# Recurrent attention and sparse-FFN layer: two staging buffers for the attention weights, and a down projection that reads its fp32 weights in both sweeps without the bf16 copy in HBM

## What is computed

```python
xn = layernorm(x)
q, k, v = split(xn @ w_atten.T); q, k = rope(q), rope(k)
s = softmax(causal(q @ k.T / sqrt(128))) @ v  @ w_proj.T
h = silu(xn @ w_gate) * (xn @ w_up)
h = keep the 2 largest magnitudes of every 4 neighbours of h
g = silu(h @ w_down)
out = x + s * g
```

## Time and profile before

| | us |
|---|---|
| median of the 2 runs | 4018.79 (3956.82 and 4080.75) |
| the profiled execution | 3956.59 |
| its span on the slowest core (core 7) | 3955.1 |
| spans of the eight cores | 3916.9 to 3955.1 |
| TensorE busy | 2852.7 (72%) |
| VectorE busy | 1323.3 (33%) |
| granted TensorE clock, mean | 0.862 |
| moved by DMA | 433.41 MB, 109 GB/s over the span |

### The profile page before, as it was taken

How to read it: one execution, slowest core, us unless ns; L and a number is a source line. 1 busy time by engine, 2 the same in 40 slices (tenths; PEclk the granted TensorE clock), 3 DMA queues, 4 the chain that set the end, 5 groups by cost and what they waited for, 6 DMA issues and landing times.

```text
span 3955.1 us, 34701 instructions; the slowest of 8 cores (3916.9 to 3955.1 us)
## 1 busy us (share of the span) xinstructions
PE 2852.7 (72%) x12592; PEld 1212.2 (31%) x12592; DVE 1323.3 (33%) x2055; ACT 603.4 (15%) x1102; POOL 263.6 (7%) x308
## 2 busy tenths in 40 slices
PE   2287879787878787847589898888898144444598
PEld 0041414242423233213234343334343022221243
DVE  4631312223131313110265665656656111111000
ACT  1112122222212121301011111111111000000000
POOL 0000000000000000001000000100101011111001
PEclk7698989898989888879899999999999577777799
DMA  5210110202020201052655555556461788887886
GB/s 161 76 52 29 42 47 23 68 2 68 3 67 3 67 5 44 4 190 97 156 128 140 144 123 130 132 121 156 115 157 42 213 212 211 212 212 178 200 194 157
DMA packets 638887, 433.41 MB, mean 110 GB/s; under 512 B 139648, under 2 KB 598400, under 8 KB 638336
## 3 DMA queue, kind: packets, MB, share of 16 engines
q1 hardware_dynamic: 612352, 343.09, 34.0%
q0 software_dynamic: 26368, 88.10, 8.2%
HBM read 359.86 MB, written 71.30 MB: 109 GB/s over the span
## 4 chain that ended last, share of the span: by engine, by line
PE 45%; DMA 30%; DVE 14%; issue 6%; SPq 3%; ACT 2%; DVEq 0%; ACTq 0%; POOLq 0%
DMA arena<-wd 13%; PE ps L689 11%; PE ps L345 7%; PE ps L395 6%; DMA d_hT<-arena 5%; PE ps L441 4%; PE ps L797 4%; DMA arena<-d_wdb 4%; PE ps L458 3%; PE ps L464 3%; PE ps L429 3%; DVE arena L476 3%; SPq L66 3%; PE ps L533 2%; DMA arena<-wvT 2%
## 5 line engine op out<-in xcount | busy, mean ns | idle before, releaser
L689 PE MATMUL ps<-arena 128*128 128x512 bf16 x4096 | 959.0, 393 | 34.4 <-DVE arena L665 24.4
L797 PE MATMUL ps<-arena 128*128 128x512 bf16 x2048 | 490.9, 403 | 387.2 <-DVE arena L774 324.5
L689 PEld LDWEIGHTS ps<-arena 128*128 128x128 bf16 x4096 | 411.1, 102 | 527.9 <-issue 90.6
L345 PE MATMUL ps<-arena 128*128 128x512 bf16 x1536 | 378.5, 403 | 58.7 <-DVE arena L325 58.7
L797 PEld LDWEIGHTS ps<-arena 128*128 128x128 bf16 x2048 | 209.8, 103 | 668.0 <-issue 451.0
L476 DVE RECIPROCAL arena<-ps 1x512 f32<-1x512 f32 x32 | 107.1, 3346 | 755.5 <-PE ps L458 755.5
L445 ACT ACTIVATE arena<-ps 128x512 bf16<-128x512 f32 x384 | 229.3, 597 | 314.4 <-PE ps L441 310.1
L345 PEld LDWEIGHTS ps<-arena 128*128 128x128 bf16 x1536 | 156.0, 102 | 274.8 <-issue 113.8
L395 PE MATMUL ps<-arena 128*128 128x256 bf16 x2048 | 231.7, 274 | 0.0
L819 DVE TENSOR_TENSOR arena<-arena 128x512 f32<-128x512 f32 x32 | 22.2, 693 | 614.8 <-DMA arena<-d_s 347.7
L395 PEld LDWEIGHTS ps<-arena 128*128 128x128 bf16 x2048 | 203.3, 99 | 27.8
(11 more groups left out here) (71 smaller groups left out, 1839.8 us busy)
## 6 DMA issues: line engine op xcount, KB each, us to landing
arena<-wgu SPq DMA_DIRECT2D x128, 1024.0 KB, 15.1
arena<-wd SPq DMA_DIRECT2D x32, 2048.0 KB, 29.5
d_wdb<-arena POOLq DMA_DIRECT2D x16, 2048.0 KB, 18.8
arena<-d_wdb SPq DMA_DIRECT2D x16, 2048.0 KB, 15.5
arena<-xT SPq DMA_DIRECT2D x4, 4096.0 KB, 14.5
arena<-wkT SPq DMA_DIRECT2D x8, 2048.0 KB, 8.8
arena<-wvT SPq DMA_DIRECT2D x8, 2048.0 KB, 8.8
arena<-wqT SPq DMA_DIRECT2D x8, 2048.0 KB, 8.7
```

The lines of the kernel that those rows point to most:

```text
L345: tok = E("tensor", lambda e, f=f, h2=h2, bank=bank, tile=tile, wv_=wv_: e.matmul(ps[bank][:], wv_[:, f, h2 * 128:(h2 + 1) * 128], xnv[:, ...
L689: tok = E("tensor", lambda e, f=f, tc=tc, bank=bank, gv=gv: e.matmul(ps[bank][:], xnv[:, f, tc * 128:(tc + 1) * 128], gv[:, f, :], start=( ...
L797: tok = E("tensor", lambda e, ic=ic, bank=bank, wdv=wdv: e.matmul(ps[bank][:], wdv[:, ic, :], hTv[:, ic, :], start=(ic == 0), stop=(ic == ...
```

## The change

It has two parts.

**Attention weights.** The one staging buffer becomes two (`wstag2`), used in turn (`(3g + wi) % 2`), each with its own `stag_free` entry. `wfree` becomes the last projection matmul of each kind instead of the last TensorE instruction of the group. Waits on `stag_free` in the output projection become waits on both entries.

**Down projection.** Both sweeps now load the fp32 weights and cast them; the bf16 copy `d_wdb` is neither written nor read. The two staging buffers become three, used in turn (`(2 fc + hf) % 3`).

```diff
-    wstag = A.alloc(NF * 256)
+    wstag2 = [A.alloc(NF * 256) for _ in range(2)]
...
+            sl = (3 * g + wi) % 2
+            t_l = kb.dma("sync", wstag2[sl][:].rearrange("p (c d) -> p c d", d=256),
+                         srcw, sem,
+                         [stag_free.get(sl)] + (xn_done if g == 0 else []))
+            t_c = E("vector", lambda e, wbf=wbf, sl=sl: e.tensor_copy(
+                wbf[:], wstag2[sl][:]), [t_l, wfree[nm]], "DVE")
+            stag_free[sl] = t_c
...
-        wfree = {"q": group_pe_tail, "k": group_pe_tail, "v": group_pe_tail}
+        wfree = {"q": q_last_mm, "k": k_last_mm, "v": v_last_mm}
...
-    wd_st2 = [A.alloc(NIC * 64) for _ in range(2)]
+    wd_st2 = [A.alloc(NIC * 64) for _ in range(3)]
...
-            if sweep == 0:
+            if True:
...
+                    hfs = (2 * fc + hf) % 3
                     t_wl = kb.dma("sync",
-                                  wd_st2[hf][:].rearrange("p (c d) -> p c d", d=128),
-                                  srcw, "dWD0" if hf == 0 else "dWD1",
-                                  [wdst_free.get(hf)] + (ph4a_tail if fc == 0 else []))
+                                  wd_st2[hfs][:].rearrange("p (c d) -> p c d", d=128),
+                                  srcw, ["dWD0", "dWD1", "dWDB0"][hfs],
+                                  [wdst_free.get(hfs)] + (ph4a_tail if sweep == 0 and fc == 0 else []))
...
-                        [t_wl, wd_read.get(fc - 2), wd_spill.get(fc - 2),
-                         ph4a_tail[2] if fc < 2 else None], "DVE")
-                    wdst_free[hf] = t_c
+                        [t_wl, wd_read.get(fc - 2),
+                         ph4a_tail[2] if sweep == 0 and fc < 2 else None], "DVE")
+                    wdst_free[hfs] = t_c
...
-                t_ws = kb.dma("gpsimd", wdbv[:, :, fc * 128:(fc + 1) * 128],
-                              wd_b[par][:].rearrange("p (c d) -> p c d", d=128),
-                              "dWDS0" if par == 0 else "dWDS1", casts)
-                wd_spill[fc] = t_ws
-            else:
-                t_wc = kb.dma("sync",
-                              wd_b[par][:].rearrange("p (c d) -> p c d", d=128),
-                              wdbv[:, :, fc * 128:(fc + 1) * 128],
-                              "dWDB0" if par == 0 else "dWDB1",
-                              [wd_spill[14], wd_spill[15], wd_read.get(fc - 2)])
```

More of the change, by code:

```diff
@@ L306, in build_nc @@
     wfree = {"q": None, "k": None, "v": None}
-    stag_free = None
+    stag_free = {}
     kv_read_tok = None
@@ L319, in build_nc @@
         toks_w = {}
[L320 to L327, removed]
+        for wi, (wap, wbf, nm, sem) in enumerate(
+                ((wkT, wk_bf, "k", "dW0"), (wvT, wv_bf, "v", "dW1"),
+                 (wqT, wq_bf, "q", "dW2"))):
+            srcw = wap[:, g * 256:(g + 1) * 256].rearrange("(c p) d -> p c d", p=128)
+            sl = (3 * g + wi) % 2
[5 more added lines that the diff above has]
+            stag_free[sl] = t_c
             toks_w[nm] = t_c
@@ L352, in build_nc @@
             t_p = tok
+            if kind == "k":
+                k_last_mm = t_p
+            else:
+                q_last_mm = t_p
             slot = ui % 2
@@ L402, in build_nc @@
             t_vp = tok
+            v_last_mm = t_vp
             t_ve = E("scalar", lambda e, tc=tc, bank=bank: e.copy(
@@ L494, in build_nc @@
         kv_read_tok = group_pe_tail
-        wfree = {"q": group_pe_tail, "k": group_pe_tail, "v": group_pe_tail}
-        t_wc_last = stag_free
+        wfree = {"q": q_last_mm, "k": k_last_mm, "v": v_last_mm}
     ph2_tail_pe = kv_read_tok
@@ L508, in build_nc @@
     t_yb = kb.dma("sync", yav, d_y[:, :].rearrange("(c p) x -> p c x", p=128), "dYB",
-                  y_spills + [ph2_tail_pe, ph2_tail_dve, ph2_tail_act, stag_free])
+                  y_spills + [ph2_tail_pe, ph2_tail_dve, ph2_tail_act,
+                              stag_free.get(0), stag_free.get(1)])
     s_spills = []
@@ L519, in build_nc @@
                       "dWP0" if par == 0 else "dWP1",
-                      [stag3_free] + ([ph2_tail_pe, ph2_tail_dve, ph2_tail_act, stag_free]
+                      [stag3_free] + ([ph2_tail_pe, ph2_tail_dve, ph2_tail_act,
+                                       stag_free.get(0), stag_free.get(1)]
                                       if cs4 == 0 else []))
@@ L747, in build_nc @@
     hTv = hT_sb[:].rearrange("p (c x) -> p c x", x=512)
-    wdbv = d_wdb[:].rearrange("p (c x) -> p c x", x=C)
-    wd_spill = {}
     wd_read = {}
@@ L769, in build_nc @@
                               fc * 128:(fc + 1) * 128].rearrange("(c p) d -> p c d", p=128)
+                    hfs = (2 * fc + hf) % 3
                     t_wl = kb.dma("sync",
-                                  wd_st2[hf][:].rearrange("p (c d) -> p c d", d=128),
-                                  srcw, "dWD0" if hf == 0 else "dWD1",
-                                  [wdst_free.get(hf)] + (ph4a_tail if fc == 0 else []))
-                    t_c = E("vector", lambda e, par=par, hf=hf: e.tensor_copy(
+                                  wd_st2[hfs][:].rearrange("p (c d) -> p c d", d=128),
+                                  srcw, ["dWD0", "dWD1", "dWDB0"][hfs],
+                                  [wdst_free.get(hfs)] + (ph4a_tail if sweep == 0 and fc == 0 else []))
+                    t_c = E("vector", lambda e, par=par, hf=hf, hfs=hfs: e.tensor_copy(
                         wd_b[par][:].rearrange("p (c d) -> p c d", d=128)
                         [:, hf * (NIC // 2):(hf + 1) * (NIC // 2), :],
-                        wd_st2[hf][:].rearrange("p (c d) -> p c d", d=128)),
-                        [t_wl, wd_read.get(fc - 2), wd_spill.get(fc - 2),
-                         ph4a_tail[2] if fc < 2 else None], "DVE")
-                    wdst_free[hf] = t_c
+                        wd_st2[hfs][:].rearrange("p (c d) -> p c d", d=128)),
+                        [t_wl, wd_read.get(fc - 2),
+                         ph4a_tail[2] if sweep == 0 and fc < 2 else None], "DVE")
+                    wdst_free[hfs] = t_c
                     casts.append(t_c)
                 t_wc = casts[-1]
-                t_ws = kb.dma("gpsimd", wdbv[:, :, fc * 128:(fc + 1) * 128],
-                              wd_b[par][:].rearrange("p (c d) -> p c d", d=128),
-                              "dWDS0" if par == 0 else "dWDS1", casts)
-                wd_spill[fc] = t_ws
-            else:
-                t_wc = kb.dma("sync",
-                              wd_b[par][:].rearrange("p (c d) -> p c d", d=128),
-                              wdbv[:, :, fc * 128:(fc + 1) * 128],
-                              "dWDB0" if par == 0 else "dWDB1",
-                              [wd_spill[14], wd_spill[15], wd_read.get(fc - 2)])
             wdv = wd_b[par][:].rearrange("p (c d) -> p c d", d=128)
```

## The result

The changed kernel takes 0.9702 of the time before (95% interval 0.9666 to 0.9739), 3.0% less. The medians are 3899.93 us of eleven runs and 3949.91 us of ten; they contain executions in which one die ran at a lower clock, and the ratio is made from the others. The profiled execution is 3829.32 us, against 3956.59 before.

What follows compares the result with a forecast made beforehand. Sweep 0 of the down projection was taken as transfer-bound, sweep 1 nearly TensorE-bound. With chunk period P = 26.0 us: 3956.6 - 90 + 30 x 26.0 - 726.2 = 3920.4 us; 8-in-10 range 3836 to 4016.

Steps and rivals of the forecast that it cites:

- part 1, attention: Attention: loading wk and wv a group ahead lets wq issue earlier, closing TensorE's hole; minus 90 us, bounds 75 and 97.
- 30 P - 726.2: Down projection: change in time in us, where P is the period from chunk to chunk, the same in both sweeps.
- P = 26.0: Down projection: chunk period in us from transfers, 23.8 for wd at 176 GB/s plus 2.2 for s, x and output.
- the 20 named as the sign: Attention: TensorE's idle for L369 was to fall below 20 us in all, from 94.4 us.
- Rival D: Attention: the hole moves to the next rope instead of closing; time 4010 us; chance 0.04.
- 176 GB/s: Down projection: rate assumed for 512 B rows of wd, read from wgu loads between 1900 and 1972 us.
- The mechanism of the chain: Down projection: a chunk waits for its casts, queued on VectorE behind the previous chunk's L819 and L823; 23.8 us per chunk.
- Rival C: Down projection, sweep 1: constant fp32 reads of 512 B rows push the rate below 158 GB/s; 4085 us; chance 0.10.
- rival B: Down projection: the engines' chain binds, period 23.8 us or less; 3854 us, or 3779 at full clock; chance 0.22.
- The 182 GB/s: Down projection: rate between 3104 and 3133 us, said to be with three wd loads queued and nothing else.
- the cross-check of 23.5: Down projection: chunk period of 23.5 us from sweep 0's queue shares at 85.6% DMA time; the prediction trusted 26.0 more.
- the estimate of 13.9 us: Down projection: a chunk's transfers, 4.98 MB at the skill's 358 GB/s, leaving the engines' chain to set the period.

Runs made afterwards that it cites:

- The kernel with early casts: Whole change, but VectorE casts chunk fc+1 ahead of chunk fc's product and sum; against the kernel before: ratio 0.9485, period 20.3 to 22.3 us.
- kernel with 8 matmuls a chunk: Whole change with casts ahead of product and sum, but 8 instead of 64 down-projection matmuls per chunk, all transfers kept: 3773.95 us, one execution.
- one-pass kernel: Changed attention; down projection holds all h in SBUF, loads and casts each weight chunk once for both token halves, casts early; ratio 0.8855 to the kernel before.

## Why the prediction was wrong

The forecast was within 2% and the measurement says 3.0% faster. By terms, as means over the cores of the two profiled executions:

| term | predicted | measured |
|---|---|---|
| part 1, attention | -90 | -95 |
| gate and up | 0 | -35 |
| down stage, 30 P - 726.2 | +54 (P = 26.0) | 0 (P = 23.9) |
| the rest | 0 | -4 |
| sum | -36 | -133 |

**Part 1: right, in mechanism and size.** Timeline of attention group 1 on core 5 after:

```profile
378.77 4.50 DVE L328 CAST arena<-arena 128x4096 bf16<-128x4096 f32 x2
381.13 0.37 SPq L66 DMA_DIRECT2D arena<-wqT  x1
391.74 2.29 DVE L328 CAST arena<-arena 128x4096 bf16<-128x4096 f32 x1 [8.48 <-DMA arena<-wqT]
395.38 0.38 PE L370 MATMUL ps<-arena 128*128 128x512 bf16 x1 [1.93 <-DVE arena L376]
395.60 3.62 PE L348 MATMUL ps<-arena 128*128 128x512 bf16 x16
```

The casts of wk and wv run together, wq is issued when the cast of wk ends, and the swap matmul starts at 395.38 (394.9 was worked out) instead of 406.13. The hole is 1.93 us instead of 11.49 (0.2 was worked out), and the unit behind it takes 3.62 us instead of 4.95. The waits, first of VectorE at L328, then for L376 (L369 before):

```profile
  DMA arena<-wqT: 65.8, 8
  DMA arena<-wkT: 13.6, 1
  DMA arena<-wvT: 3.4, 1
...
  PE ps L370: 20.8, 15
```

73.1 us of `wvT` became 3.4, and 94.4 us for L369 became 20.8, just above the 20 named as the sign. The attention part alone takes 80 and 91 us off this stage in its two profiles. Rival D, the hole that moves, is out.

**Part 2: the step that failed is the rate of the transfers, 176 GB/s, and with it P = 26.0.** The formula 30 P - 726.2 held to 9 us: with the measured 23.9 it gives -9, and the stage changed by 0. The mechanism of the chain was right, and so was its size: 23.8 was worked out, and the period is 23.82 to 23.93 on every core and in both sweeps. That it fits to 0.1 us is in part luck. The terms of the prediction add up to 23.9, not 23.8, and count 0.26 us twice, since the 17.0 us from a cast's end to the Silu hold the step to the first matmul already; without it they give 23.7, and short waits between the instructions make up the rest. Rival C is out: sweep 1 keeps the period of sweep 0. One chunk on core 5 after:

```profile
3205.20 16.67 PE L796 MATMUL ps<-arena 128*128 128x512 bf16 x64 [7.22 <-DVE arena L783]
3222.02 0.60 ACT L806 ACTIVATE arena<-ps 128x512 f32<-128x512 f32 x1 [23.30 <-PE ps L796]
3222.86 0.69 DVE L818 TENSOR_TENSOR arena<-arena 128x512 f32<-128x512 f32 x1 [17.92 <-ACT arena L806]
3223.72 0.69 DVE L822 TENSOR_TENSOR arena<-arena 128x512 f32<-128x512 f32 x1 [0.17 <-DVE arena L818]
3224.33 4.50 DVE L783 CAST arena<-arena 128x4096 bf16<-128x4096 f32 x2
3229.09 16.67 PE L796 MATMUL ps<-arena 128*128 128x512 bf16 x64 [7.22 <-DVE arena L783]
```

Both casts run without a wait between them (4.50 us for two), right behind L822, and TensorE starts with their end: 16.67 + 7.22 = 23.89. Over the kernel, L783 waited for, and who waited for it:

```profile
  DMA arena<-wd: 90.4, 4
...
  PE ps L796: 323.4, 32
```

That is the sign that the prediction had named for rival B: TensorE's wait is for the casts alone, and VectorE waits for `wd` only four times, for the two loads of the first chunk of each sweep; it is 32 and 4 on all eight cores. The kernel with early casts shows the other side: the loads could come every 20 to 22 us. The difference between 26.0 and 23.9 is 63 us of time, and rival B's 3854 us was the time to forecast for this part.

Why was the rate too low? The figure in the sum, 176 GB/s, is that of another tensor, `wgu`, in another stage: the rows of both have 512 B, but those of `wgu` lie 64 KB apart and those of `wd` 8 KB. It is no oddity of core 7: the 72 us from 5 us after a core's first `wgu` issue, which on core 7 are 1900 to 1972, bring the eight cores 168 to 189 GB/s, a mean of 180. So the step from one tensor to the other failed. What makes the two rates differ, the distance of the rows or what else TensorE and the queues do in that stage, no run here shows.

The 182 GB/s that seemed to confirm it were read on `wd`, but on core 7 alone, the slowest core, whose trace one looks at first. Here are the packets of the kernel before on cores 0 to 7, each from the landing of its h to the landing of the second `wd` load, with nothing but `wd` under way:

```profile
DMA packets 8237, 4.20 MB, mean 241 GB/s; under 512 B 32, under 2 KB 8237, under 8 KB 8237
DMA packets 8543, 4.36 MB, mean 197 GB/s; under 512 B 32, under 2 KB 8543, under 8 KB 8543
DMA packets 7911, 4.03 MB, mean 183 GB/s; under 512 B 32, under 2 KB 7911, under 8 KB 7911
DMA packets 8460, 4.32 MB, mean 233 GB/s; under 512 B 32, under 2 KB 8460, under 8 KB 8460
DMA packets 8239, 4.20 MB, mean 239 GB/s; under 512 B 32, under 2 KB 8239, under 8 KB 8239
DMA packets 7817, 3.99 MB, mean 197 GB/s; under 512 B 32, under 2 KB 7817, under 8 KB 7817
DMA packets 7903, 4.03 MB, mean 219 GB/s; under 512 B 32, under 2 KB 7903, under 8 KB 7903
DMA packets 9390, 4.79 MB, mean 181 GB/s; under 512 B 32, under 2 KB 9390, under 8 KB 9390
```

In each pair (0 and 1, 2 and 3, 4 and 5, 6 and 7) one core gets 219 to 241 GB/s and its neighbour 181 to 197. The stretches are 17 to 26 us long, and by the time of its own span the faster core of each pair comes to this place 7 to 11 us later than its neighbour, so the slower one starts while the faster one still loads h. But where both are past their h, for 12 to 15 us, the split is as wide (264 against 197, 269 against 178, 264 against 197, 225 against 173), so what makes it stays open. Core 7 has the lowest rate of all. There were never more than two `wd` loads under way at a time, not three as the prediction says. The mean of the eight is 211 GB/s, and with it the transfers need 4.19 / 0.211 + 2.2 = 22.1 us: below the chain's 23.8, and inside the 20.1 to 22.9 us of the two kernels that measured it. So rows that could have been read before gave the right answer. So did the cross-check of 23.5, also below the chain, which the prediction set aside.

The Trainium skill ("DMA: Bandwidth & Descriptors", Specifications) has 512 B as the smallest size at line rate. It pointed to rival B, which came true, but the estimate of 13.9 us for a chunk's transfers, worked out from that page's 358 GB/s, did not: 20.1 us is the least measured here, on eight cores with rows of 512 B.

**Gate and up: counted at nothing, it gave 35 us.** The prediction took each stage that the change doesn't touch as fixed, without a reason. But this stage is not bound by one engine. With half of its loads left out it is 68 to 75 us shorter, so its length moves with what the transfers happen to get. The traces show where. VectorE copies the transposed h out of PSUM (L637, L647 after) and there waits for the write of an earlier piece of h to HBM, since that frees the buffer; TensorE's transposes (L631, L641) then wait for the selection behind it (L614, L624). These two waits on core 4 before, after, and with half of the `wgu` loads:

```profile
  DVE arena L614: 136.5, 94
  DMA d_hT<-arena: 29.3, 15
...
  DVE arena L624: 121.0, 102
  DMA d_hT<-arena: 11.8, 7
...
  DVE arena L614: 95.2, 106
  DMA d_hT<-arena: 2.8, 1
```

As means over the cores, TensorE's wait goes from 145 to 119 us, and to 95 with half of the loads; VectorE's wait for the write goes from 37 to 18 and to 3. Most of the rest of the 35 us is TensorE itself: inside the stage it is busy for 974 us before and 965 after, at a clock of 0.958 and 0.971. Over the 96 cores of the twelve profiles with all loads, the length of the stage follows VectorE's wait for the write with a correlation of 0.84. That is not a proof of cause, since both may follow the transfers.

How an earlier stage moves this one is not settled, nor how much of the 35 us belongs to the change: the groups of profiles differ by 24 us in the mean, and on one chip by 11. The notion that the two cores of a pair then run further apart, and get in each other's way less, fits the means: by their own spans they start this stage 27 us apart with the attention part (10 to 42) and 13 without (0.5 to 35). But within each group distance and length hardly go together (a correlation of -0.04 and -0.16).

**The third buffer and the copy.** The prediction gave the third buffer the role of keeping P at bytes over rate. As the chain bound, it was worth little (12 us in the stage). Nor did the part as a whole pay: alone it is 1.000, and together with the attention part it has a down stage of 815 us where the old code has 800 and 807. Whether that costs a whole percent of the time is not settled: the ratios (0.9598 without part 2, against 0.9702) say so, the repetition on another chip (3848.7 us, 2% less than before there) does not. The bytes are the same in both (16 writes and 16 reads of 2.1 MB against 32 reads more). Sweep 0 went from 32.7 to 33.7 us a chunk down to 23.9, and sweep 1 from 15.0 to 15.5 up to 23.9: 9 us won and 9 us lost.

## What to carry to other kernels

Take a transfer rate from loads of the same tensor, and read it on all cores before a sum hangs on it: another tensor's rate with the same row size was 180 GB/s against 211, and a short stretch on one core was up to 14% off the mean. Where an in-order engine has preparation work for the next step queued behind consumers of this step, work out that chain first and reorder it before adding buffers: here the order was worth 61 us and the third buffer 12. And before moving bytes between two passes over the same weights, ask whether one pass fits: it took 343 us off a stage in which both ways of doing two passes took the same 815, and 282 off the two passes with early casts.

## What the runs showed of the hardware that was not expected

- While the first two `wd` loads of sweep 0 ran, one core of each pair moved 219 to 241 GB/s and the other 181 to 197. The Trainium skill ("HBM Reference", Specifications (TRN2)) says that both cores of a pair share the bandwidth of their HBM. One high and one low in each pair fits that, but no run here has a core alone; that the shares are uneven for 12 us and more is what these rows add.
- In the kernel with 8 matmuls a chunk all eight cores kept 217 to 248 GB/s each over whole sweeps, in which 84% of the bytes came in rows of 512 B, 8 KB apart.
- The granted clock after is 0.79 in both sweeps, where TensorE is busy 16.67 us of every 23.9. It was 0.74 in the old sweep 0, with 16.3 of 33.7, and 0.97 in the old sweep 1 and in the one-pass kernel, where TensorE has hardly a gap. The idle costs twice, since a chunk behind a gap starts at the lower clock. The first 4.0 and the last 8.7 us of the chunk at 3205.2 above, with the time of a matmul in them, 0.63 us at 0.50 (1.2 GHz) and 0.38 at 1.00 (2.4 GHz), are below (columns as in the earlier trace rows). So 64 matmuls take 16.67 us there and 14.25 in the old sweep 1.

```profile
3205.20:3209.20 4.00, 4.00 (x10) 1.42 (x11) 0.00 (x0) 0.00 (x0) 0.39 (x1) 0.50 0.94 237
3213.20:3221.90 8.70, 8.67 (x40) 3.71 (x38) 0.00 (x0) 0.00 (x0) 0.00 (x0) 1.00 1.01 264
```

- A stage of 4096 matmuls that no edit touched took 1069 to 1115 us in the mean from profile to profile, and 1041 with half of its loads.
